# Three weight sums per pair in a Strassen feed-forward kernel: on VectorE instead of GpSimd

## The reference

```python
y   = zX * lap_x(x) + zY * lap_y(x) + zR * x * (1 - x)        # five-point stencil, reflecting edges
m1  = (even[:, :4, :, None] * odd[:, :4, None, :]).reshape(8, 2048, 512)   # from 16 tokens of y
m2  = (even[:, 4:, :, None] * odd[:, 4:, None, :]).reshape(8, 512, 2048)
h   = y @ W1.T + scale * (y @ m1.T) + b1
out = x + gelu(h) @ W2.T + scale * (gelu(h) @ m2.T) + b2
```

## Time and profile before

| | us |
|---|---|
| median of three runs | 1340.38 |
| lowest, highest | 1339.84, 1341.73 |
| the profiled execution | 1341.16 |
| its span | 1339.4 |
| TensorE busy | 1333.8 |
| VectorE busy | 1036.4 |
| ScalarE busy | 794.2 |
| GpSimd busy | 273.3 |

### The profile page before, as it was taken

How to read it: one execution, slowest core, us unless ns; L and a number is a source line. 1 busy time by engine, 2 the same in 40 slices (tenths; PEclk the granted TensorE clock), 3 DMA queues, 4 the chain that set the end, 5 groups by cost and what they waited for, 6 DMA issues and landing times.

```text
span 1339.4 us, 17071 instructions
## 1 busy us (share of the span) xinstructions
PE 1333.8 (100%) x5878; PEld 1100.8 (82%) x5878; DVE 1036.4 (77%) x1761; ACT 794.2 (59%) x1370; POOL 273.3 (20%) x272
## 2 busy tenths in 40 slices
PE   9999999999999999999999999999999999999998
PEld 7887888888888888888888888888888888888887
DVE  8887799957898588976899768996689967665343
ACT  6654557645776457755577546675467754666432
POOL 1013222301333012320123201331022310232000
PEclk9999999999999999999999999999999999999999
DMA  7764288777777677775778767686767867676661
GB/s 243 189 160 150 53 213 215 205 202 196 191 205 207 204 209 192 198 209 180 209 194 222 188 203 208 190 216 177 228 180 203 214 183 204 161 191 164 172 196 48
DMA packets 140070, 253.52 MB, mean 189 GB/s; under 512 B 13648, under 2 KB 37456, under 8 KB 139984
## 3 DMA queue, kind: packets, MB, share of 16 engines
q1 hardware_dynamic: 122032, 201.43, 46.9%
q0 software_dynamic: 17376, 49.29, 21.9%
q10 hardware_dynamic: 576, 1.72, 0.3%
HBM read 189.34 MB, written 63.05 MB: 188 GB/s over the span
## 4 chain that ended last, share of the span: by engine, by line
PE 98%; DVE 1%; DMA 1%; POOL 0%; ACT 0%; issue 0%; POOLq 0%; DVEq 0%; SPq 0%
PE po L634 17%; PE po L636 17%; PE po L635 17%; PE ph L618 15%; PE ph L620 15%; PE ph L622 15%; PE ph L610 1%; DMA W2s<-in_w_dram 0%; PE ph L628 0%; PE po L590 0%; PE ph L661 0%; DVE W2l L1297 0%; DMA X<-in_xT_dram 0%; PE po L703 0%; DVE xr L1353 0%; PE ph L604 0%
## 5 line engine op out<-in xcount | busy, mean ns | idle before, releaser
L634 PE MATMUL po<-W2h,gh 128*128 128x512 f32 x1020 | 396.9, 389 | 0.8 <-DVE gl L1346 0.8
L636 PE MATMUL po<-W2h,gl 128*128 128x512 f32 x1020 | 396.8, 389 | 0.0
L635 PE MATMUL po<-W2l,gh 128*128 128x512 f32 x1020 | 396.8, 389 | 0.0
L618 PE MATMUL ph<-yh,W1h 128*128 128x512 f32 x896 | 348.6, 389 | 0.0
L620 PE MATMUL ph<-yl,W1h 128*128 128x512 f32 x896 | 348.6, 389 | 0.0
L622 PE MATMUL ph<-yh,W1l 128*128 128x512 f32 x896 | 348.5, 389 | 0.0
L634 PEld LDWEIGHTS po<-W2h,gh 128*128 128x128 f32 x1020 | 191.4, 188 | 40.9 <-issue 1.2
L636 PEld LDWEIGHTS po<-W2h,gl 128*128 128x128 f32 x1020 | 191.4, 188 | 39.8
L635 PEld LDWEIGHTS po<-W2l,gh 128*128 128x128 f32 x1020 | 191.4, 188 | 39.7
L618 PEld LDWEIGHTS ph<-yh,W1h 128*128 128x128 f32 x896 | 168.2, 188 | 35.1 <-DVE W1l L1239 0.2
L622 PEld LDWEIGHTS ph<-yh,W1l 128*128 128x128 f32 x896 | 168.2, 188 | 34.9
(11 more groups left out here) (122 smaller groups left out, 1388.7 us busy)
## 6 DMA issues: line engine op xcount, KB each, us to landing
W2s<-in_w_dram SPq DMA_DIRECT2D x124, 256.0 KB, 3.8
R<-in_w_dram POOLq DMA_DIRECT2D x62, 512.0 KB, 7.4
uv_scratch<-UVs SPq DMA_DIRECT2D x112, 256.0 KB, 4.2
UVs<-uv_scratch SPq DMA_DIRECT2D x112, 256.0 KB, 3.8
X<-in_xT_dram SPq DMA_DIRECT2D x56, 390.0 KB, 4.4
xr<-in_x_dram SPq DMA_DIRECT2D x16, 1024.0 KB, 5.5
xr<-in_b_dram POOLq DMA_DIRECT2D x16, 1024.0 KB, 10.9
out_dram<-xr SPq DMA_DIRECT2D x64, 256.0 KB, 2.4
```

Source lines behind the costliest of these rows:

```text
L618: e.matmul(bank[:, :], W1h[:, f, blk, wc], yh[:, q, c, :], start=first and c == 0, stop=False, skip_group_check=not first)
L634: e.matmul(po[t][:, :], gh[:, lt, st], W2h[:, k, :], start=i == 0 and lt == 0, stop=False)
L635: e.matmul(po[t][:, :], gh[:, lt, st], W2l[:, k, :], start=False, stop=False)
L636: return e.matmul(po[t][:, :], gl[:, lt, st], W2h[:, k, :], start=False, stop=i == NI - 1 and lt == 1)
```

## The change

The functions top0, top1 and top3 move from GpSimd's list to VectorE's, unchanged in what they compute and wait for. In the first half VectorE runs top0 and top1 in front of w1lB(b, i+1), and top3 behind it. The three of the next batch's first pair stand, at the end of the batch, between c22(b, 7) and glL(b, 1, 6). GpSimd keeps its DMA issues.

```diff
@@ -518,24 +518,6 @@
                 e.wait_ge(s_outer, summed(b, i))
                 e.dma_start(flat(R1[:, f, :, :]), w1[i], accum_op=ALU.add).then_inc(d_r[f], 16)
 
-            def top0(b, i):
-                f = i % 2
-                if (b, i) > (1, 0):
-                    pb, pi = (b, i - 1) if i else (b - 1, 7)
-                    e.wait_ge(d_td, 16 * strassen(pb, pi))
-                    e.wait_ge(s_w1lT, strassen(pb, pi))
-                e.wait_ge(d_r[f], added(b, i))
-                e.tensor_tensor(Ts[:, 0:4:2, :], R1[:, f, 0:1, :].broadcast_to([128, 2, 256]), R1[:, f, 1:3, :],
-                                ALU.subtract).then_inc(s_top0, 1)
-
-            def top1(b, i):
-                e.wait_ge(s_top0, strassen(b, i))
-                e.tensor_tensor(Ts[:, 1, :], Ts[:, 0, :], R1[:, i % 2, 2, :], ALU.subtract).then_inc(s_top1, 1)
-
-            def top3(b, i):
-                e.wait_ge(s_top1, strassen(b, i))
-                e.tensor_tensor(Ts[:, 3, :], Ts[:, 1, :], R1[:, i % 2, 3, :], ALU.add).then_inc(s_top3, 1)
-
             def add_b2(b, h):
                 e.wait_ge(d_xr, 16 * (2 * b + h + 1))
                 e.dma_start(xr[:, :, :], bass.AP(b2.tensor, 0, [[0, 128], [0, 4], [1, D]]),
@@ -560,24 +542,14 @@
             side(1, 7)
             token(1, 7)
             add_W1(1, 1)
-            top0(1, 0)
-            top1(1, 0)
-            top3(1, 0)
             add_b2(0, 1)
             for b in range(1, B):
-                for i in range(7):
-                    top0(b, i + 1)
-                    top1(b, i + 1)
-                    if i < 6:
-                        add_W1(b, i + 2)
-                    top3(b, i + 1)
+                for i in range(6):
+                    add_W1(b, i + 2)
                 add_b2(b, 0)
                 add_b2(b, 1)
                 if b + 1 < B:
                     add_W1(b + 1, 0)
-                    top0(b + 1, 0)
-                    top1(b + 1, 0)
-                    top3(b + 1, 0)
                     add_W1(b + 1, 1)
 
         @block.tensor
@@ -1296,6 +1268,24 @@
                 e.wait_ge(s_w2h, tiles2(b, n))
                 e.tensor_tensor(W2l[:, k, :], w2s_at(b, n), W2h[:, k, :].bitcast(f32), ALU.subtract).then_inc(s_w2l, 1)
 
+            def top0(b, i):
+                f = i % 2
+                if (b, i) > (1, 0):
+                    pb, pi = (b, i - 1) if i else (b - 1, 7)
+                    e.wait_ge(d_td, 16 * strassen(pb, pi))
+                    e.wait_ge(s_w1lT, strassen(pb, pi))
+                e.wait_ge(d_r[f], added(b, i))
+                e.tensor_tensor(Ts[:, 0:4:2, :], R1[:, f, 0:1, :].broadcast_to([128, 2, 256]), R1[:, f, 1:3, :],
+                                ALU.subtract).then_inc(s_top0, 1)
+
+            def top1(b, i):
+                e.wait_ge(s_top0, strassen(b, i))
+                e.tensor_tensor(Ts[:, 1, :], Ts[:, 0, :], R1[:, i % 2, 2, :], ALU.subtract).then_inc(s_top1, 1)
+
+            def top3(b, i):
+                e.wait_ge(s_top1, strassen(b, i))
+                e.tensor_tensor(Ts[:, 3, :], Ts[:, 1, :], R1[:, i % 2, 3, :], ALU.add).then_inc(s_top3, 1)
+
             def w1lB(b, i):
                 f = i % 2
                 e.wait_ge(s_w1hB, 8 * b + i)
@@ -1468,6 +1458,9 @@
                     sum3(1)
                     part_l(1, 4)
             glL(0, 1, 6)
+            top0(1, 0)
+            top1(1, 0)
+            top3(1, 0)
             w1lB(1, 0)
             sums(2, 0)
             mul(2, 0)
@@ -1502,7 +1495,10 @@
                         part_l(1, 5)
                     if i == 1:
                         part_l(b, 6)
+                    top0(b, i + 1)
+                    top1(b, i + 1)
                     w1lB(b, i + 1)
+                    top3(b, i + 1)
                     if (b, i) > (1, 0):
                         w2l(b, 2 * i + 4)
                     fold(b, 2 * i + 5, 0, 1)
@@ -1527,7 +1523,10 @@
                     tile(b + 1, 7)
                 glL(b, 0, 5)
                 c11(b, 6)
+                top0(b, 7)
+                top1(b, 7)
                 w1lB(b, 7)
+                top3(b, 7)
                 w1lT(b, 7)
                 glE(b, 0, 6)
 
@@ -1589,6 +1588,10 @@
                     elif nxt:
                         w1lB(b + 1, 0)
                     c22(b, i)
+                    if i == 7 and nxt:
+                        top0(b + 1, 0)
+                        top1(b + 1, 0)
+                        top3(b + 1, 0)
                     glL(b, 1, i - 1)
                     if i in (5, 7) and nxt2:
                         fin(b + 2, (i - 5) // 2)
```

## The result

The changed kernel takes 1349.64 us in the median of four runs (1348.81 to 1349.85), the kernel before 1340.11 us (1339.3 to 1341.73): 1.0067 of the time before, interval 1.0056 to 1.0079, so 7.5 to 10.6 us slower. Predicted were 1348.5 us. The profiled execution took 1348.81 us with a span of 1347.1, 7.7 us more than that of before, 1341.16 and 1339.4.

A forecast was written before the change was run, and what follows sets the result against it. TensorE's gapless queue of matmuls was taken as the bound. Boundary stalls of 3.1 us and second-pair stalls of 4.7 and 0.3 us made 8.1 us on 1340.4 us: 1348.5 us, range 1342.5 to 1356.5 us.

The forecast's parts named there:

- What bounds: TensorE is busy 1333.8 of 1339.4 us, matmuls without gaps; changes to other engines can win at most about a microsecond.
- The price of the sums: On VectorE, the three sums delay its queue by 0.73, 0.34 and 0.34 us: 1.41 us per pair, 79 us over 56.
- What is given back: VectorE's W2l and y operations, no longer slowed beside GpSimd's sums, regain 2.2 us per pair; VectorE's load falls a little.
- Stall 1: At the six batch boundaries TensorE waits for glL, now behind the sums: 0.51 us each, 3.1 us in all.
- Stall 2: In a batch's second pair TensorE waits for cpV behind late w1hT: 0.94 us in five batches, 0.3 us in the first.
- What keeps its cover: From the third pair on, a round of 12.1 us against TensorE's 12.25 us: spare 0.1 to 0.3 us, no repeated stall.
- the stall recurs: Third to fifth pairs stall 0.1 to 0.3 us each, boundary and second pair 0.3 us more: 1355.5 us, chance 0.15.

The follow-up runs named there:

- all three places mended: Changed kernel with part_l(b, 6) at the second pair's end, boundary loads ahead of store_T, glL and ghL ahead of the boundary's sums and w1hT: 1341.03 us, 0.9999.
- the mended orders: Changed kernel with ScalarE's w1hT behind cpV, 1347.48 us; the same with the boundary's glL and ghL also ahead of sums and w1hT, 1352.15 us.
- part_l late: Changed kernel with part_l(b, 6) moved from in front of the second pair's sums to that pair's end: 1344.22 us, 1.0028.
- the run without waits: Changed kernel whose second and third sums read only weight quarters, so VectorE waits for none of its own results; result not right: 1346.93 us, 1.0042.
- the run with zeros: Kernel before, with GpSimd filling the three tiles with zeros in place of the sums: 1340.57 us, 1.0003.

## Why the prediction was right, point by point

- What bounds: TensorE without gaps, so that the change could only lose. Right; the kernel with all three places mended, with VectorE undisturbed by sums on GpSimd, is at 0.9999.
- The price of the sums: 0.68, 0.42 and 0.42 us predicted, 0.683, 0.426 and 0.418 measured. The first delays the second by 0.71 to 0.72 us (predicted 0.73), the third is complete 2.35 us after the first's start in a pair (predicted 2.36). The Trainium skill (VectorE: DVE Perf Modes, section The DRAIN you can't avoid) says, from eight copies, that the semaphore costs nothing extra; the runs differ, with starts 0.71 and 0.46 us apart with a wait and 0.60 and 0.33 us without.
- What is given back: W2l takes 0.702 us in the mean over all now, beside a sum it took 1.46. Behind batch 0 W2l is never above 0.69 us now and y never above 0.76, as foretold. But I said that VectorE's load would fall a little, and it rose from 1036.4 to 1042.1 us. The sums add 85.4 us there, so what came back is 79.7 us, 1.4 us per pair and not 2.2: that figure was read at a place with all three operations under a sum. GpSimd keeps 96.2 us where I said below 90; before, its groups add up to 288 us against 273.3 us busy, so they overlap, and leaving out the sums takes less than their own time away. Neither number stood in the sum.
- Stall 1: predicted 0.51 us six times, measured 0.44. The mis-sized term is the time from glL's end to TensorE's start, 0.15 us taken from the wait in batch 0 and 0.06 us here; the first matmuls lose 0.11 us more instead of 0.08. The batch 0 place was not a like one: TensorE's list has two waits in front of that matmul (for W2l and for glL), and only the one for glL at the boundary.
- Stall 2: predicted 0.94 us five times and 0.3 us once, measured 1.09 to 1.25 and 0.36. By itself it is 0.80 us, less than predicted by some 0.06 us at TensorE's start again, 0.04 us of VectorE's lateness and small steps; 0.3 to 0.45 us come from the EB1 load behind store_T, which I had named and given 0 to 0.5 us, in the range only and nothing in the sum. The errors have opposite signs: without the EB1 load the stalls would add up to 7.0 us, and it brings 1.7 us. That the sum of 8.1 us lies so near the 8.7 us measured in waits is luck in part. The 0.3 us for b = 1 was a guess between 0 and 0.94.
- What keeps its cover: the round of the third and later pairs held, no stall there. How thin it is no run shows: in the mended orders a third pair stalled, but no later one did.
- The rival "the stall recurs" had one thing right, the late EB1, which makes the second pairs' stall longer. Its other half, a round longer than TensorE's, did not come: in no run does a pair behind the third stall.
- Not foreseen: that a second cover lies behind the first, so that taking w1hT out of cpV's way would give back 2 us and not 7.

## What to carry to other kernels

When one engine is the bound and never waits, cost a move of work by where its results are due, not by the busy time of the engine that gets it: 79 us of sums on VectorE cost nothing here once three orders were mended, and the stalls of 8.7 us came from one item of 1.1 us in front of them, from a store in front of a load, and from two handovers in a row at the batch boundary. Mend such orders together: with part_l late and the store still in front of the loads, the boundary's order took away 2.6 us of waits and brought 6.6. Follow each moved result through every in-order queue that waits for it, DMA queues included, and after one late handover look for the next: the first stall hides it.

## What the runs showed of the hardware

- VectorE waiting for its own preceding result costs 0.11 to 0.13 us against no wait (starts 0.60 and 0.33 us apart in the run without waits, 0.71 and 0.46 us in the changed kernel).
- A GpSimd operation that only writes SBUF leaves VectorE's W2l at 0.69 us (the run with zeros); beside a sum of GpSimd, which reads SBUF, it took 1.46 us.
- How TensorE starts again depends on the place. Where its list has one wait in front of the matmul (glL at a boundary, cpV, glE, W1l in batch 0), it starts 0.05 to 0.06 us after the releasing engine's end, and the next matmul 0.34 us later instead of 0.227. Where it has two or more in a row (w1lT and cpP in front of p6 in the mended orders, W2l and glL in batch 0), it starts 0.14 to 0.15 us after, and the next matmul 0.31 us later. This holds for all 62 and 31 such waits behind the first 40 us of the traces; no run changes the number of waits alone, so it is not shown that the number is the cause.
- Batch 0, whose matmuls and their order are the same in all these kernels, has gaps between matmuls near 45 and 108 us that differ from one profiled execution to the next: 1.1 us in all before, 0.6 us with part_l late, 1.9 us with all three places mended. A microsecond of any comparison here is that.
